# A fused two-layer transformer kernel: one stretch ordered anew by key tile, with the queries' squares kept whole

## The reference

```
x = x + softmax_attention(layernorm(x), ctx)     # 16 heads of 128, 4 KV heads, RMS norm of q and k
x = x + moe0(layernorm(x))
x = x + linear_attention(layernorm(x), ctx)      # 16 heads of 16, 64 features relu(k @ Wkf.T)
x = x + moe1(layernorm(x))
```

```
q  = rms_norm(layernorm(x) @ Wq) * weights       # for each of 16 heads: mean of q*q over 128, then q * rsqrt(mean + eps)
k  = ctx @ Wk1.T + bk ;  v = ctx @ Wv1.T + bv    # layer 1, all 8 contexts of 1500 rows
kp = relu(k @ Wkf.T) * mask
kv[h] = sum over rows of kp[h] x [v[h], 1]       # 64 x 17 sums of each head and context
```

## Time and profile before

| | us |
|---|---|
| median of 3 runs | 1410.51 (1408.31 to 1410.95) |
| the profiled execution's own time | 1409.69 |
| its span, first to last instruction | 1407.9 |
| TensorE busy | 1237.1 (88%) |
| VectorE busy | 890.0 (63%) |
| ScalarE busy | 739.2 (53%) |
| GpSimd busy | 539.0 (38%) |
| mean granted clock of TensorE | 0.943 |

### The profile page before, as it was taken

The page is one execution under the profiler, slowest core; times in us unless marked ns, Lnnn a source line. Parts: engine busy times, 40 slices in busy tenths (PEclk is TensorE's granted clock), DMA queues, the critical chain, the costliest instruction groups (busy, mean ns, idle before and its releaser), DMA issues. The chain is left out here.

```text
span 1407.9 us, 27107 instructions
## 1 busy us (share of the span) xinstructions
PE 1237.1 (88%) x9559; PEld 1059.3 (75%) x9559; DVE 890.0 (63%) x1859; ACT 739.2 (53%) x1262; POOL 539.0 (38%) x560
## 2 busy tenths in 40 slices
PE   5888888888886999999999999999999767978697
PEld 4777777777773888888888888888888656855585
DVE  4654455455454778787888887787886494442543
ACT  3544545444453666657666665766756323431542
POOL 1422222222223635465353545536363061512452
PEclk9999999999997999999999999999999877987799
DMA  4111101101003111101111110111000050005000
GB/s 144 39 31 50 39 15 51 37 19 47 8 2 88 44 45 44 46 3 41 44 44 44 33 54 0 44 44 44 0 0 1 29 199 1 1 0 205 1 0 14
DMA packets 38748, 56.05 MB, mean 40 GB/s; under 512 B 3058, under 2 KB 37154, under 8 KB 38178
## 3 DMA queue, kind: packets, MB, share of 16 engines
q1 hardware_dynamic: 38226, 54.82, 12.2%
q10 hardware_dynamic: 464, 0.46, 0.1%
HBM read 54.81 MB, written 0.46 MB: 39 GB/s over the span
## 5 line engine op out<-in xcount | busy, mean ns | idle before, releaser
L1094 POOL TENSOR_TENSOR att_sq<-att_work,att_sq 128x500 fp32r<-128x500 f32 x96 | 127.1, 1324 | 180.9 <-DVE att_sq L992 180.9
L1099 POOL TENSOR_TENSOR att_k<-att_work,att_k 128x500 fp32r<-128x500 f32 x96 | 129.7, 1351 | 159.5 <-DVE att_k L1000 159.5
L101 PE MATMUL att_csum<-att_pT,att_cn 125*128 125x448 f32 x384 | 155.0, 404 | 1.4 <-DVE att_pT L1038 0.4
L544 DVE SCALAR_TENSOR_TENSOR kvs_ks<-kvs_keys_ps,kvs_bk,kvs_ks 64x500 fp32r<-64x500 f32 x96 | 70.8, 738 | 134.6 <-ACT kvs_ks L456 133.0
L352 PE MATMUL kvs_feat<-kvs_f,kvs_ks 128*125 128x256 f32 x768 | 117.6, 291 | 31.6 <-DVE kvs_kp L599 15.9
L916 ACT ACTIVATE att_pr<-att_pr,att_nmx 112x1500 f32<-112x1500 f32 (+1 forms) x96 | 108.6, 1131 | 67.6 <-DVE att_nmx L1029 67.6
L103 PE MATMUL att_csum<-att_pT,att_cn 125*128 125x448 f32 x384 | 140.1, 365 | 0.0
L102 PE MATMUL att_csum<-att_pT,att_cn 125*128 125x448 f32 x384 | 139.3, 363 | 0.0
L456 ACT ACTIVATE kvs_ks<-kvs_keys_ps,kvs_bk 64x500 fp32r<-64x500 f32 x96 | 64.9, 676 | 140.5 <-PE kvs_keys_ps L103 139.1
L1038 DVE TENSOR_TENSOR att_pT<-att_ring,att_pT 125x448 fp32r<-125x448 f32 x192 | 118.4, 617 | 22.6 <-ACT att_pT L932 22.4
L352 PEld LDWEIGHTS kvs_feat<-kvs_f,kvs_ks 128*125 128x125 f32 x768 | 101.4, 190 | 40.3 <-issue 28.5
(11 more groups left out here) (254 smaller groups left out, 3316.5 us busy)
## 6 DMA issues: line engine op xcount, KB each, us to landing
attention_raw_t<-in_ctxT SPq DMA_DIRECT2D x45, 500.0 KB, 4.1
att_raw_n<-in_ctx SPq DMA_DIRECT2D x16, 750.0 KB
w_gate<-in_gate SPq DMA_DIRECT2D x1, 2112.0 KB, 9.8
w_up<-in_up SPq DMA_DIRECT2D x1, 2112.0 KB, 14.6
kvs_raw_q<-in_wq SPq DMA_DIRECT2D x8, 256.0 KB, 2.8
wo_raw<-in_wo SPq DMA_DIRECT2D x4, 512.0 KB, 6.6
w_down<-in_down SPq DMA_DIRECT2D x1, 2048.0 KB, 18.3
w_gate<-in_gate SPq DMA_DIRECT2D x1, 1760.0 KB, 13.4
```

The lines of the kernel that those rows point to most:

```text
L101: nc.tensor.matmul(out, w_lo, x_hi, start=start, stop=False, skip_group_check=True)
L544: nc.vector.scalar_tensor_tensor(ks[64:128, c, 2 * m + h, :], keys_ps[y, 0:CH], bk[y, m:m + 1], ks[0:64, c, 2 * m + h, :].bitcast(F32), AL ...
L1094: nc.gpsimd.tensor_tensor(sq[1][:, i % 2, :], work[:, i % 2, :], sq[0][:, i % 2, :].bitcast(F32), ALU.subtract).then_inc(sq_lo, 1)
L1099: nc.gpsimd.tensor_tensor(k[1][x], work[:, i % 2, :], k[0][x].bitcast(F32), ALU.subtract).then_inc(k_lo, 1)
```

## The change

All of it is in `sums_and_queries`.

- `sq` is one float32 tile that ScalarE's square writes directly, and `mean_mat` is float32. The mean is one plain float32 matmul. VectorE's rounding and GpSimd's subtraction of the square, with their semaphores, are gone.
- Heads 2i and 2i+1 are done in step i at t = 4 and 8, in every step; square, mean and root follow one, two and three tiles later. `project` also waits on `mean_free`.
- A moves from t = 1, 4, 7, 10 to t = 2, 5, 8, 11.
- `take_sums` moves to t = 3; `turn` and `read_blocks` move to t = 4.
- `split` moves from the end of the chunk to its second tile (n = 1), `split_heads` to t = 1.
- In step 0 all `xn` are done at t = 0, `turn_x` at t = 1, the splits of `xnT` at t = 2 and 3, the norm weights at t = 5, `wk0` and `wv0` at t = 6 and 10.

The core of the diff:

```diff
-        mean_mat = p.sb("mean_mat", [128, 128], F32R)
+        mean_mat = p.sb("mean_mat", [128, 128])
-        sq = [p.sb(f"sq{i}", [128, 2, NTOK], F32R) for i in range(2)]
+        sq = p.sb("sq", [128, 2, NTOK])
...
-        SQUARE_AT, MEAN_AT, ROOT_AT = 1, {False: 3, True: 2}, {False: 4, True: 2}
+        SQUARE_AT, MEAN_AT, ROOT_AT = 1, 2, 3
...
-        def queries_at(i, first, last, t, after):
-
-            if first:
-                return []
-            heads = {0: (0, 2 * (i - 1)), 6: (1, 2 * (i - 1) + 1)} if not last else \
-                {3 * n: (n % 2, NH - 4 + n) for n in range(4)}
-            return [heads[t - after]] if t - after in heads else []
+        def queries_at(i, t, after):
+
+            return [(n, 2 * i + n) for n in range(2) if t - after == 4 + 4 * n]
...
                 wait(pe, q_lo, pair + 1)
                 wait(pe, proj_free, h + 1)
+                wait(pe, mean_free, h + 1)
...
-                wait(pe, sq_lo, h + 1)
+                wait(pe, sq_done, h + 1)
                 wait(pe, mean_free, h + 1)
-                for half in (1, 0):
-                    last = nc.tensor.matmul(mean[:, 0:NTOK], mean_mat[:], sq[half][:, k, :],
-                                            start=(half == 1), stop=(half == 0))
-                last.then_inc(mean_done, 1)
+                nc.tensor.matmul(mean[:, 0:NTOK], mean_mat[:], sq[:, k, :], start=True, stop=True).then_inc(mean_done, 1)
...
-                        if t % GROUP == 1:
-                            if t > 1:
+                        if t % GROUP == GROUP - 1:
+                            if t >= GROUP:
                                 add(i, t // GROUP - 1)
                             elif not first:
                                 add(i - 1, NG - 1)
                         if n in (0, 2) and to_project is not None:
                             keys(*to_project, n // 2)
-                        if t == 2 and not first:
+                        if t == 4 and not first:
                             turn(i - 1)
-                        if first and t == 4:
+                        if first and t == 1:
                             turn_x()
...
-                nc.scalar.activation(work[:, k, :], proj[:, 0:NTOK], ACT.Square, bias=zero[:, 0:1]).then_inc(sq_done, 1)
+                nc.scalar.activation(sq[:, k, :], proj[:, 0:NTOK], ACT.Square, bias=zero[:, 0:1]).then_inc(sq_done, 1)
...
-                        if t == 2 and not first:
+                        if t == 3 and not first:
                             take_sums(i - 1)
...
+                        if n == 1 and to_split is not None:
+                            split(*to_split)
+                        if t == 1:
+                            split_heads(i)
...
-                    if to_split is not None:
-                        split(*to_split)
...
-            def round_square(h, k):
-
-                wait(dve, sq_done, h + 1)
-                nc.vector.tensor_copy(sq[0][:, k, :], work[:, k, :]).then_inc(sq_hi, 1)
...
-                        if t == 2 and not first:
+                        if t == 4 and not first:
                             read_blocks(i - 1)
...
                         if first and t == 0:
                             sharpen()
-                        if first and t < TT:
-                            nc.vector.tensor_scalar(xn[:, t, :], x[:, t, :], mv[:, t, 0:1], rstd[:, t:t + 1],
-                                                    ALU.subtract, ALU.mult).then_inc(xn_done, 1)
+                            for y in range(TT):
+                                nc.vector.tensor_scalar(xn[:, y, :], x[:, y, :], mv[:, y, 0:1], rstd[:, y:y + 1],
+                                                        ALU.subtract, ALU.mult).then_inc(xn_done, 1)
...
-            def split_square(h, k):
-
-                wait(pool, sq_hi, h + 1)
-                nc.gpsimd.tensor_tensor(sq[1][:, k, :], work[:, k, :], sq[0][:, k, :].bitcast(F32),
-                                        ALU.subtract).then_inc(sq_lo, 1)
```

More of the change, by code:

```diff
@@ L245, in sums_and_queries @@
             "q_loaded", "q_hi", "q_lo", "nw_loaded", "nw_done"))
-        proj_done, proj_free, sq_done, sq_hi, sq_lo, mean_done, mean_free, rs_done = (p.sem(s) for s in (
-            "proj_done", "proj_free", "sq_done", "sq_hi", "sq_lo", "mean_done", "mean_free", "rs_done"))
+        proj_done, proj_free, sq_done, mean_done, mean_free, rs_done = (p.sem(s) for s in (
+            "proj_done", "proj_free", "sq_done", "mean_done", "mean_free", "rs_done"))
         block = ctx.enter_context(nc.Block())
         NG = KT // GROUP
-        SQUARE_AT, MEAN_AT, ROOT_AT = 1, {False: 3, True: 2}, {False: 4, True: 2}
+        SQUARE_AT, MEAN_AT, ROOT_AT = 1, 2, 3
         def context(i):
@@ L424, in step @@
                             keys(*to_project, n // 2)
-                        if t == 2 and not first:
+                        if t == 4 and not first:
                             turn(i - 1)
-                        if first and t == 4:
+                        if first and t == 1:
                             turn_x()
-                        for k, h in queries_at(i, first, last, t, MEAN_AT[last]):
+                        for k, h in queries_at(i, t, MEAN_AT):
                             mean_square(h, k)
-                        for k, h in queries_at(i, first, last, t, 0):
-                            project(h, k, i - 1 if not last else h // 2)
+                        for k, h in queries_at(i, t, 0):
+                            project(h, k, i)
             pe.wait_ge(w_lo, 2)
@@ L497, in step @@
                             keys(*to_project, n // 2)
-                        for k, h in queries_at(i, first, last, t, SQUARE_AT):
+                        for k, h in queries_at(i, t, SQUARE_AT):
                             square(h, k)
-                        for k, h in queries_at(i, first, last, t, ROOT_AT[last]):
+                        for k, h in queries_at(i, t, ROOT_AT):
                             root(h, k)
-                        if first and t in (5, 6):
-                            act.wait_ge(turned_done, t - 4)
-                            nc.scalar.activation(xnT[0][:, t - 5, :], (proj, mean)[t - 5][:, 0:NTOK], ACT.Copy)\
+                        if n == 1 and to_split is not None:
+                            split(*to_split)
+                        if t == 1:
+                            split_heads(i)
+                        if first and t in (2, 3):
+                            act.wait_ge(turned_done, t - 1)
+                            nc.scalar.activation(xnT[0][:, t - 2, :], (proj, mean)[t - 2][:, 0:NTOK], ACT.Copy)\
                                 .then_inc(x_hi, 1)
-                        if first and t in (9, 10):
+                        if first and t in (6, 10):
                             act.wait_ge(a_loaded, 32)
[L508 to L512, removed]
-                    if to_split is not None:
-                        split(*to_split)
+                            w = t // 10
+                            nc.scalar.activation((wk0, wv0)[w][0][:], raw_a[:, w], ACT.Copy).then_inc(a_hi, 1)
             nc.scalar.dma_start(x[:], a["x"].rearrange("(t p) d -> p t d", p=TP)).then_inc(x_loaded, 16)
@@ L602, in step @@
                             keys(*to_project, n // 2)
-                        if t == 2 and not first:
+                        if t == 4 and not first:
                             read_blocks(i - 1)
-                        for k, h in queries_at(i, first, last, t, SQUARE_AT):
-                            round_square(h, k)
-                        for k, h in queries_at(i, first, last, t, ROOT_AT[last]):
+                        for k, h in queries_at(i, t, ROOT_AT):
                             normalise(h, k)
@@ L610, in step @@
                             sharpen()
-                        if first and t < TT:
-                            nc.vector.tensor_scalar(xn[:, t, :], x[:, t, :], mv[:, t, 0:1], rstd[:, t:t + 1],
-                                                    ALU.subtract, ALU.mult).then_inc(xn_done, 1)
[L614 to L619, removed]
+                            for y in range(TT):
+                                nc.vector.tensor_scalar(xn[:, y, :], x[:, y, :], mv[:, y, 0:1], rstd[:, y:y + 1],
+                                                        ALU.subtract, ALU.mult).then_inc(xn_done, 1)
+                        if first and t in (2, 3):
+                            dve.wait_ge(x_hi, t - 1)
+                            nc.vector.tensor_tensor(xnT[1][:, t - 2, :], (proj, mean)[t - 2][:, 0:NTOK],
+                                                    xnT[0][:, t - 2, :].bitcast(F32), ALU.subtract)\
+                                .then_inc((proj_free, mean_free)[t - 2], 1)
+                        if first and t == 5:
                             dve.wait_ge(nw_loaded, 32)
@@ L627, in _ @@
```

(12 more changed lines are left out.)

## The result

The changed kernel takes **1352.55 us** (median of 4, 1351.42 to 1353.69) against 1410.73 before: ratio 0.9591, 95% interval 0.9574 to 0.9607, 58.2 us less. Its profiled execution took 1353.69 us, with a span of 1352.0, and is the slowest of the four.

A forecast was written before the change was run, and what follows sets the result against it. TensorE's work in `sums_and_queries`, with its waits and half clock, was taken to set the time. Steps 1 to 6 -54, step 0 +7, last step -11.7 sum to -58.7 on 1409.69 us: forecast 1351, own range 1345 to 1359.

The forecast's parts named there:

- A: A group's sums on TensorE, priced at 1.46 us from start to start at full clock.
- the signs named for "right": Steps 1 to 6: no L659 key waits, L561 waits about 1.0, L599 waits at tiles 2 and 4 only, clock 1.0.
- those for "wrong": Clock 0.94 again, a step over 44 us, waits for ScalarE's features, or a stage ending later than 375 us.
- 12 V+F, 4 A, 6 K, 2 P, 2 M, a turn: TensorE us: V+F values and features 1.66, A group's sums 1.46, K half keys 1.46/1.37, P projection 1.23, M head's mean 0.41.
- the account of before: Old steady step: 38.4 us of work, 9.9 of waits, 2.7 of half clock make 51.0, against 51.15 measured.
- Splits: At tiles 1, 5, 9, three tiles ahead of their keys; two waits a step gone, 1.53 and 1.36 recorded.
- Waits for VectorE at tiles 2 and 4, and `kv_done` at 5: New TensorE waits in a steady step: 0.82+0.82+0.97 and three restarts of 0.1, 3.0 us a step.
- +0.34 a head: Plain float32 mean on TensorE: taken at 0.75 us instead of 0.41 for each head.
- the rival that priced cheap means at -5.4: Mean at its low end (-5.4) and step 0 without collision (-2.5): 1343 us, chance 0.06.
- the rival in which it falls as before (1370): TensorE's clock falls as often as before, so 19 us come back: 1370 us, chance 0.15.
- its written terms (4.0 + 3.4 - 0.9 + 2.5 + 1 - 1.7): Step 0: two heads +4.0, turns' wait 3.4 less 0.9, collision 2.5, clock 1, waits gone 1.7; sum +7.
- The collision of `xn` with GpSimd: Step 0, tile 0: VectorE's `xn` stretched beside GpSimd subtractions; bounds 0 and 3.6 us, taken at 2.5.

The follow-up runs named there:

- run 7: Changed kernel with sums' end earlier, norm of x ahead of the first keys, and first head at tile 3 with its square at 5: 1329.20 us.
- Runs 3: Changed kernel with the context splits back at the end of a chunk (fourth tile instead of second): 1409.72 us.
- run 4: Kernel before with only the context splits moved to the second tile of their chunk: 1373.57 us.
- run 5: Changed kernel with a context's last sums group at tile 1, copy at 2, turn and `read_blocks` at 3: 1337.57 us.
- run 8: Changed kernel with only the first head's projection moved from tile 4 to 3 and its square to 5: 1362.69 us.
- run 1: Changed kernel with the queries' squares in halves again, two float32r matmuls for the mean: 1350.15 us.
- run 2: Kernel before with only the plain float32 mean of undivided squares, its order kept: 1397.38 us.
- Run 6: Changed kernel with the Newton steps and four `xn` moved from tile 0 of step 0 to ahead of the first keys: 1345.65 us.

## Why the prediction was right

**The forecast** was 1351, measured 1352.55. The sum was formed on the profiled execution, which fell by 56.0 us where 58.7 were forecast. Step by step, between the two profiled executions:

| | forecast | measured |
|---|---|---|
| step 0 | +7 | +7.7 |
| steps 1 to 6 | -54 | -55.6 |
| last step | -11.7 | -9.1 |
| stages behind | 0 | +1.1 |
| span | -58.7 | -55.9 |

So steps 1 to 6, where most of the gain was placed, carry it. In steps 1 to 6 all the signs named for "right" are there, and none of those for "wrong". Part of the closeness is luck, since errors of 0.7 to 2.6 us stand in every part and the one in steps 1 to 6 offsets some of the others.

**The account of a step.** The listed prices (12 V+F, 4 A, 6 K, 2 P, 2 M, a turn) add up to 37.6 us, not 38.4, so the account of before closed with 0.9 a step unexplained. The total was nevertheless good: run 7's steps, without a wait, take 39.07, and less the 0.68 for two plain means that is 38.4. So 0.8 a step is missing from the list and not from the total; the changed order contains it too, so it hardly touches the difference. The prediction also read a 9 in the slices of the clock as "not at full"; a full clock prints the same digit, and the 0.94 of the table by step is what showed the loss.

**Splits.** Right: no key waits for L659 in steps 1 to 6. Runs 3 and 4 show their weight, which the prediction had not set apart: within the new order 57 of the 58 us go without them, in the old one they give 62%. The parts don't add up, since the new order without them has more and longer waits for the same split (46.2 us in 23 waits) than the old one (22.3 in 15). No run moved the heads or the sums (A, turn, `read_blocks`) alone, so their share of the gain is not shown.

**Waits for VectorE at tiles 2 and 4, and `kv_done` at 5.** Right in place and size (0.86, 0.86, 1.0 against 0.82, 0.82, 0.97 forecast); run 5 takes two of them away by moving VectorE's work, and run 7 the third. Runs 7 and 8 together say that order decides: with `read_blocks` at tile 4 the head at tile 3 makes a step 0.3 us longer (42.2) at full clock and brings back the falls of the clock; with `read_blocks` at tile 3 it makes a step 1.0 shorter (run 7 against run 5). In both it costs a wait of 2.9 in step 0.

**The mean.** The price was right (0.537 a record), and as an item of the new stream so was +0.34 a head. What it does not say is what the plain mean is worth: run 1, with the halves back, is 2.4 us faster and not 5.4, because without the longer mean a wait comes back at the first head. So the rival that priced cheap means at -5.4 took too much. In the old order the plain mean is a gain (run 2).

**The clock.** Forecast full in steps 1 to 6, and 1.00 there; the rival in which it falls as before (1370) lost. The kernel before stood at 0.94 with 47 waits in six steps, all but one of them under 1.6 us; the changed one has 18, of 0.6 to 0.9. The Trainium skill (TensorE: Matmul & The Clock Gate, section "A second HAM failure mode: psum-queue depth-cycling") says that short idles, if frequent enough, make the clock swing. The kernel before agrees with that; the changed kernel's three idles are, by its 1.00, too few or too short for it. Run 8 has only two a step, one of 0.6 and one of 2.05, and its clock falls in four of six steps, in or right behind the long one: so the length of an idle counts, or the sum of them (2.65 instead of 2.04), and not the number alone. No run here parts these two.

**Step 0.** The forecast of +7 is near the +7.7, but its written terms (4.0 + 3.4 - 0.9 + 2.5 + 1 - 1.7) add up to 8.3, or to 5.8 if the collision is meant inside the 3.4; the 7 is a choice between them. The collision of `xn` with GpSimd, taken at 2.5, came to 2.7 (4.34 for four where 1.64 would do). The half clock was taken at 1: the clock of step 0 is 0.90 instead of 0.96, 7 us more at half clock, at most 3.1 at 0.45 each. Run 6 takes the turns' wait and this half clock away together and gains 6.9.

**The last step** fell 2.6 short. Three gaps there have no semaphore behind them (1.00, 0.51 and 1.47, which the profile calls issue), 3.0 together, enough to account for it. Before, this step shows none on TensorE, though it was written out there too. What they are stays open; no run tested it. The 1.1 us of the later stages go with the clock: by the trace's clock records 120 us of them stand at half clock after the change and 112 before, and in runs 2 and 8, with 104, these stages took 978.0 instead of 979.3 before. Why the clock differs in stages that nobody changed is open.

## What to carry to other kernels

Price an added item by what it puts into the bounding engine's queue beyond the wait behind it; a dearer matmul in front of a wait can be free, and a cheaper one can buy nothing. When an order is laid anew, look one item past each removed wait for the in-order engine that is late next: here the same head at tile 3 made a step 0.3 us longer and brought the falls of the clock back, or made it 1.0 shorter, by where `read_blocks` stood. Look at the first step by itself too: there that head cost a wait of 2.9 either way. Work that another engine prepares belongs ahead of its use by its full chain: here moving two calls was worth 36 us.

## What the runs showed of the hardware

Short idles cost clock besides their own length. With the plain mean alone (run 2) TensorE's recorded waits in steps 1 to 6 fell by 5.5 us and 17 us less of the stage stood at half clock. Lengthening one idle a step from 0.85 to 2.05, with another removed (run 8), made the steps 0.3 us longer, and those in which the clock fell (four of six) another 1.3 to 1.6. A fall cost 1.5 us in run 4 as well.

Of four `xn` on VectorE (SBUF to SBUF), 0.41 us alone, the two that started beside GpSimd's subtractions took 2.42 and 1.35, each ending 0.15 behind one. VectorE's reads of PSUM kept their 0.48 and 0.69 beside such subtractions, before and after the change.
